# The first attention block of a four-layer kernel: queries and keys before the values' weights, values behind the first scores

## The reference, cut to what matters

```python
def _L0_attn_ref(x, Wq, Wk, Wv):
    ...
    Q = (x @ Wq.T).reshape(b, n, H, R)
    K = (x @ Wk.T).reshape(b, n, H, R)
    V = (x @ Wv.T).reshape(b, n, H, d)
    attn = jnp.einsum('bnhr,bmhr->bhnm', Q, K)
    attn = jax.nn.softmax(attn, axis=-1)
    out = jnp.einsum('bhnm,bmhd->bnd', attn, V)
    return out
...
x = x + _layernorm(_L0_attn_ref(_layernorm(x, axis=-1), ...), axis=-1)
x = x + _layernorm(_L0_ffn_ref(_layernorm(x, axis=-1), ...), axis=-1)
```

## Time and profile before

| | us |
|---|---|
| median of 3 runs | 1325.25 |
| lowest and highest | 1322.7, 1328.19 |
| the profiled execution | 1323.63 |
| its span in the trace | 1321.8 |
| first attention without a break on PE from | 52.9 |

### The profile page before, as it was taken

How to read it: one execution, slowest core, us unless ns; L and a number is a source line. 1 busy time by engine, 2 the same in 40 slices (tenths; PEclk the granted TensorE clock), 3 DMA queues, 4 the chain that set the end, 5 groups by cost and what they waited for, 6 DMA issues and landing times.

```text
span 1321.8 us, 21970 instructions
## 1 busy us (share of the span) xinstructions
PE 1196.8 (91%) x7921; PEld 686.2 (52%) x7921; DVE 994.1 (75%) x2058; ACT 799.6 (60%) x1585; POOL 386.1 (29%) x304
## 2 busy tenths in 40 slices
PE   6799999999999879895899999998889979799987
PEld 4366666666666634341333333343467754477653
DVE  5878978889879178777667677776689857888855
ACT  5876866767768123240466666676668862688751
POOL 0000000001000034474310000014588841698823
PEclk9899999999999989996699999998989989899999
DMA  5576857767768635562223321100111100011101
GB/s 153 127 168 151 184 136 171 168 150 159 171 139 186 155 107 129 140 193 72 76 59 96 83 43 42 39 3 22 28 29 30 36 20 0 21 34 34 30 13 32
DMA packets 62823, 119.92 MB, mean 91 GB/s; under 512 B 15522, under 2 KB 30060, under 8 KB 61324
## 3 DMA queue, kind: packets, MB, share of 16 engines
q1 hardware_dynamic: 62716, 118.53, 37.5%
HBM read 37.68 MB, written 5.57 MB: 33 GB/s over the span
## 4 chain that ended last, share of the span: by engine, by line
PE 71%; DVE 15%; ACT 5%; issue 4%; POOL 2%; DMA 2%; SPq 2%; DVEq 0%; POOLq 0%; ACTq 0%
PE ps L748 15%; PE ps L768 8%; PE ps L1068 6%; PE ps L1027 5%; PE ps L1048 4%; PE ps L1125 4%; PE ps L719 2%; PE ps L1176 2%; PE ps L1259 2%; PE ps L1198 2%; PE ps L1230 2%; ACT probsT L2257 2%; PE ps L900 2%; PE ps L1306 2%; PE ps L1241 2%
## 5 line engine op out<-in xcount | busy, mean ns | idle before, releaser
L2257 ACT ACTIVATE probsT<-ps 128x512 f32<-128x512 f32 (+1 forms) x304 | 163.9, 577 | 101.3 <-PE ps L1052 90.4
L1469 DVE TENSOR_REDUCE negmax<-ps 128x1 f32<-128x1024 f32 x128 | 153.6, 1205 | 40.0 <-PE ps L768 39.6
L2443 POOL TENSOR_SCALAR rstd<-mv 128x4 f32<-128x4 f32 (+1 forms) x31 | 7.9, 255 | 505.7 <-DVE mv L1403 505.4
L1027 PE MATMUL ps<-arena 84*128 84x512 bf16 (+3 forms) x384 | 114.9, 361 | 27.3 <-DVE cmax L1714 21.4
L768 PE MATMUL ps<-k_st,q_st 64*128 64x512 f32 x512 | 130.0, 627 | 9.7 <-ACT d_sq L2101 5.4
L2101 ACT ACTIVATE d_sq<-ps,negmax 128x1024 f32<-128x1024 f32 x86 | 96.0, 1116 | 61.4 <-DVE negmax L1469 58.7
L1714 DVE CUSTOM_DVE_ANT_0 q_st<-ps,rel 128x256 f32<-128x256 f32 (+7 forms) x128 | 96.7, 756 | 46.9 <-PE ps L1027 46.1
L1714 DVE CUSTOM_DVE_ANT_0 k_st<-ps,rel 128x256 f32<-128x256 f32 (+7 forms) x128 | 96.8, 756 | 38.7 <-PE ps L1027 37.7
L748 PE MATMUL ps<-probsT,v_nat 128*128 128x256 f32 x512 | 120.0, 388 | 5.2 <-DMA probsT<-probs 3.0
L748 PE MATMUL ps<-probsT,v_st 128*128 128x256 f32 x512 | 119.4, 385 | 0.8 <-DVE xn L1422 0.6
L1048 PE MATMUL ps<-arena 87*128 87x512 bf16 (+3 forms) x384 | 113.3, 338 | 5.5 <-ACT probsT L2257 3.3
(11 more groups left out here) (232 smaller groups left out, 2550.8 us busy)
## 6 DMA issues: line engine op xcount, KB each, us to landing
probsT<-arena SPq DMA_DIRECT2D x336, 128.0 KB, 2.4
probsT<-probs SPq DMA_DIRECT2D x176, 128.0 KB, 2.4
d_sq<-e_gates SPq DMA_DIRECT2D x16, 512.0 KB, 5.1
probsT<-probsT SPq DMA_DIRECT2D x62, 128.0 KB, 2.4
arena<-c_q_parts SPq DMA_DIRECT2D x8, 576.0 KB
arena<-c_k_parts SPq DMA_DIRECT2D x8, 576.0 KB
q_st<-e_gates SPq DMA_DIRECT2D x8, 512.0 KB, 5.1
k_st<-e_gates SPq DMA_DIRECT2D x8, 512.0 KB, 5.6
```

The lines of the kernel that those rows point to most:

```text
L1027: ins = pe.matmul(ps[:, 2 * (u % 2) + i, 0:e - i * CH], c_q2[buf][0:SHALLOW, j, qt * P:(qt + 1) * P], c_k2[buf][0:SHALLOW, j, i * CH:e], s ...
L1469: dve.tensor_reduce(negmax[:, u:u + 1], s2, AX_X, ALU.max, negate=True).then_inc(s_a_negmax, 1)
L2257: act.activation(c_p[:, kt % 2, j0:j0 + heads, q0 - kt * P:q0 - kt * P + n], ps[:, 4 + c % 2, 0:heads * n].rearrange("p (h n) -> p h n", n ...
```

## The change

The first block's order is new, all else of the kernel is untouched.

- PE no longer transposes Wv ahead of the projections. It projects the keys, then the queries, and goes to `scores(0, 0)`.
- `turn_w0(2)` and `(3)` move into the piece of slot 0, behind `scores(0, 0)`. The values' projection is split in halves, behind `scores(0, 1)` and `scores(0, 2)`; both halves go to banks 6 and 7, the second after the first is copied out.
- The scores of slots 0 and 1 of block 0 no longer wait for the values.
- `turn_f` moves: groups 0 to 3 all into slot 3, groups 4 to 7 all into slot 4, group 8 into slot 5. Group 0 also waits for the values' second half to be copied.
- DVE loses its two copies of the turned Wv and its copy of the values' second half. ACT makes them: the turned Wv in slot 0, the halves of the values in slots 1 and 2, the experts' copies in slots 3, 4 and 5.

```diff
                 if g == 0:
                     pe.wait_ge(s_ld_f, 16 * 11)
+                    pe.wait_ge(s_a_v1, 1)
...
-            def a_proj_v(m):
+            def a_proj_v(m, halves=(0, 1)):
                 b, p = m // PAIRS, m % PAIRS
-                if m > 0:
-                    pe.wait_ge(s_a_exp, NU * m)
-                for half, done in ((0, s_a_projv0), (1, s_a_projv1)):
-                    if half:
-                        pe.wait_ge(s_a_q, m + 1)
+                for half in halves:
+                    if m == 0:
+                        pe.wait_ge((s_w0t, s_a_v0)[half], (2, 1)[half])
+                    else:
+                        pe.wait_ge((s_a_exp, s_a_q)[half], (NU * m, m + 1)[half])
...
# PE: a_piece
-                if slot < 4:
-                    turn_f(2 * slot)
-                    turn_f(2 * slot + 1)
-                if slot == 4:
+                if slot == 0:
+                    pe.wait_ge(s_ld_wv, 16)
+                    turn_w0(2)
+                    turn_w0(3)
+                if slot in (1, 2):
+                    a_proj_v(0, (slot - 1,))
+                if slot in (3, 4):
+                    for g in range(4 * slot - 12, 4 * slot - 8):
+                        turn_f(g)
+                if slot == 5:
                     turn_f(8)
...
-            pe.wait_ge(s_ld_wv, 16)
-            turn_w0(2)
-            turn_w0(3)
             pe.wait_ge(s_w0a, 2)
             pe.wait_ge(s_xT, 2)
+            a_proj_k(0)
             a_proj_q(0)
-            a_proj_k(0)
-            pe.wait_ge(s_w0t, 2)
-            a_proj_v(0)
...
# DVE
-            turned_w0(0)
-            turned_w0(1)
             a_evac_k(0)
-            a_evac_v(0)
...
# ACT
+            def first_v(half):
+                act.wait_ge((s_a_projv0, s_a_projv1)[half], 1)
+                act.copy(a_v[0][:, 4 * half:4 * half + 4, :].rearrange("p (n k) c -> p n (k c)", n=2),
+                         ps[:, 6:8, :]).then_inc((s_a_v0, s_a_v1)[half], 1)
...
-                if slot < 4:
-                    turned_f(2 * slot)
-                    turned_f(2 * slot + 1)
-                if slot == 4:
+                if slot == 0:
+                    turned_w0(0)
+                    turned_w0(1)
+                if slot in (1, 2):
+                    first_v(slot - 1)
+                if slot in (3, 4):
+                    for g in range(4 * slot - 12, 4 * slot - 8):
+                        turned_f(g)
+                if slot == 5:
                     turned_f(8)
```

More of the change, by code:

```diff
@@ L708, in a_proj_k @@
                 ins.then_inc(s_a_projk, 1)
-            def a_proj_v(m):
+            def a_proj_v(m, halves=(0, 1)):
                 b, p = m // PAIRS, m % PAIRS
-                if m > 0:
-                    pe.wait_ge(s_a_exp, NU * m)
-                for half, done in ((0, s_a_projv0), (1, s_a_projv1)):
-                    if half:
-                        pe.wait_ge(s_a_q, m + 1)
+                for half in halves:
[3 more added lines that the diff above has]
+                        pe.wait_ge((s_a_exp, s_a_q)[half], (NU * m, m + 1)[half])
                     for i in range(4):
                         t = b * QT + 4 * half + i
-                        ins = pe.matmul(ps[:, pair(m, 2 + half) + i // 2, (i % 2) * 256:(i % 2) * 256 + 256],
+                        ins = pe.matmul(ps[:, (pair(m, 2 + half) if m else 6) + i // 2, (i % 2) * 256:(i % 2) * 256 + 256],
                                         xT[:, t * P:(t + 1) * P], w0v[:, p, :], start=True, stop=True)
-                    ins.then_inc(done, 1)
+                    ins.then_inc((s_a_projv0, s_a_projv1)[half], 1)
             def weigh(m, c, head, k0, k1):
@@ L757, in scores @@
                 if i == 0:
-                    for ready in (s_a_q, s_a_k, s_a_v0):
+                    for ready in (s_a_q, s_a_k):
                         pe.wait_ge(ready, m + 1)
+                    if m > 0:
+                        pe.wait_ge(s_a_v0, m + 1)
                 elif i == 1:
-                    pe.wait_ge(s_a_v1, m + 1)
+                    if m > 0:
+                        pe.wait_ge(s_a_v1, m + 1)
                     pe.wait_ge(s_a_exp, NU * m + 1)
@@ L1433, in half_xn @@
                 ins.then_inc(s_xn, 1)
[L1435 to L1439, removed]
             def a_evac_k(m):
@@ L2091, in a_evac_v, with turned_w0 @@
                 act.wait_ge(s_a_projv0, m + 1)
-                act.copy(a_v[m % 2][:, 0:4, :].rearrange("p (n k) c -> p n (k c)", n=2), ps[:, pair(m, 2):pair(m, 2) + 2, :]).then_inc(s_a_v0, 1)
+                act.copy(a_v[m % 2][:, 0:4, :].rearrange("p (n k) c -> p n (k c)", n=2),
+                         ps[:, pair(m, 2):pair(m, 2) + 2, :]).then_inc(s_a_v0, 1)
+            def first_v(half):
+                act.wait_ge((s_a_projv0, s_a_projv1)[half], 1)
+                act.copy(a_v[0][:, 4 * half:4 * half + 4, :].rearrange("p (n k) c -> p n (k c)", n=2),
+                         ps[:, 6:8, :]).then_inc((s_a_v0, s_a_v1)[half], 1)
+            def turned_w0(n):
+                act.wait_ge(s_w0p, 3 + n)
+                act.copy(w0v[:, 2 * n:2 * n + 2, :], ps[:, 6 + n, :].rearrange("p (n c) -> p n c", n=2)).then_inc(s_w0t, 1)
             def soft(m, u):
```

## The result

The changed kernel takes 1332.87 us (median of 9 runs), the kernel before 1323.26 (9 runs, the three shown above among them). The ratio is 1.0059, with a 95% interval of 1.0044 to 1.0074: slower by some 7.8 us (5.8 to 9.8).

A forecast was written before the change was run, and what follows sets the result against it. PE bounds the kernel (busy 91%), so only the first weighing's start counts: 5.6 for the holds net of the start's gain plus 2.8 for the clock make 8.4 us slower, 1325.25 + 8.4, rounded 1333.5, range 1329 to 1337.

The forecast's parts named there:

- The one number: The whole effect is how much the start of the first weighing, at 52.88 us before, moves.
- The premise: From the first weighing on, PE has work at every moment, and the change leaves that work as it is.
- The start: Projections up to the first scores: these start at 16.5 instead of 19.19 us, a gain of 2.7.
- Slots 0 to 2: The values' halves delay scores by 0.4 and 0.65, both covered; exponential of unit 6 at 35.0, gain still 2.7.
- Slots 3 and 4, the holds: PE waits for ACT's end-of-slot copies; scores of slots 4 and 5 start late; 5.3 lost by the exponential of unit 10.
- Slot 5: The weighing waits for the last small copies at the end of ACT's slot 5 and starts at 58.5 us.
- The sum without the clock: First weighing 5.6 us later if PE's clock stays at its upper level throughout.
- The clock: Two score bursts behind the idle times in slots 3 and 4 start at the lower clock: 2.8 us more.
- The upper bound: Clock cost if both bursts in slots 3 and 4 run low to their ends: 4.5 us.
- The clock did not stay up: Rival: holds in slots 3 and 4 but full clock, 5.6 us slower, 1330.9 us; chance 0.24.
- The gain at the start did not pass through: Rival claimed it would: slot 4's scores before about 37 us, first weighing 2.7 earlier, 1322.5 us; chance 0.07.
- The start did come forward: Rival claimed it would not: first scores stay where they were, 11.1 us slower, 1336.4 us; chance 0.05.

The follow-up runs named there:

- e2: The changed kernel with ACT's copies of the experts' groups moved forward in slot 4 alone: 1327.88 us, ratio 1.0022 to the kernel before.
- e5: e1 plus three matmuls that nobody reads in PE's idle time ahead of the scores of slot 6: 1320.16 us, ratio 0.9959 to the kernel before.
- e1: The changed kernel with ACT's copies of the experts' groups moved forward inside slots 3 to 5: 1322.28 us, ratio 0.9988 to the kernel before.
- e4: The changed kernel with matmuls that nobody reads in PE's idle time ahead of groups 2 and 6: 1328.67 us, ratio 1.0028 to the kernel before.

## Why the prediction was right, point by point

- **The one number.** All rests on the start of the first weighing. It moved by 8.5 (8.9 counted from PE's first transpose), the time by 7.8, forecast 8.4. That the forecast of 1333.5 lies 0.6 from the median is in part luck: it was built on 1325.25, 2.0 above the nine-run median of before, and the medians differ by 9.6.
- **The premise** that PE has work at every moment from the first weighing on is too strong. It is idle for 3.2 us of the next 340 and for 102.4 us of the rest of the span; in the changed kernel for 3.6 and 103.3. What the sum needs is only that this part doesn't change, and no run here shows that it did.
- **The start.** Forecast 2.7 at the first scores. The profile shows 3.0 net of the loads, the experiments 2.5 to 3.4 where the clock was up. The term that I had not counted is what the clock does to the start. In two of eight profiles of kernels with the new start the keys' projection took 3.75 instead of 1.95 (e2 and e5), and the gain there is only 0.9 and 0.4. The clock record begins with the rise to full speed, at 15.8 and 16.0 us in these two and at 9.6 to 11.4, ahead of the projection, in the other six. In the one profile of before it is at 12.3, just as the projections begin, so whether the old order escapes this isn't shown; nor is it shown that the 0.77 for which PE is now idle ahead of the projection plays a part, since all eight have it.
- **Slots 0 to 2.** As forecast: PE held by the values twice, no delay on ACT, exponential of unit 6 at 34.35 (forecast 35.0, 0.4 of the difference being the loads).
- **Slots 3 and 4, the holds.** Scores of slot 4 at 41.34 (41 to 42), of slot 5 at 52.44 (50 to 53), both ended by ACT's copies. e1 took the holds away and 9.4 us of time with them; e2 showed that each is half.
- **Slot 5.** The weighing at 61.40 stands 0.34 behind the start of ACT's last small copy (61.06), as in e2 (59.25 to 59.58), where that copy alone ended its wait. The scores of slot 6, low clock and all, ended at 61.35 and hid, barely.
- **The sum without the clock** was 5.6; e4 shows 5.4. With the 3.5 of the clock that makes the 8.9 of the profile, where 8.4 were forecast.
- **The clock** was the term that was too small: 2.8 taken, 3.5 measured. I had counted the low clock on the two score groups alone; the rows that I had left at full clock, the transposes released by the hold, cost 1.4 of it (0.83 + 0.61), while the second score group cost 0.83 and not 1.5. Two slips change nothing in the forecast. The upper bound takes 0.85 for six transposes where the row has 0.93. And the 1.6 and 1.7 by the Trainium skill (TensorE: Matmul & The Clock Gate, HAM oscillation) halve the whole rows of 3.26 and 3.49, where the page halves the throttled time. Of the first row only the 2.7 us from 39.56 to 42.25 are that, which gives 1.3, as measured.
- **The rivals.** The clock did not stay up. The gain at the start did not pass through: its point of decision was a start of slot 4's scores before about 37, it was 41.34. The start did come forward.

## What to carry to other kernels

When side work is packed closer on an in-order engine, look at its buffers: with two banks, the third and fourth group wait for copies of the same batch, and then everything queued behind them starts at the copier's pace. Place a copy in its engine's order by when the other engine needs the buffer back, not at the end of a stage; that alone took away the 7.8 us of loss here, and 1.6 to 2.4 of gain are left by the ratios, whose intervals end at 1.0000. And count the clock when a hold leaves TensorE idle: here the transposes and scores behind the two holds (3.96 and 5.35 us idle) ran low for the most part, which added 3.5 us to the 5.4 that the kernel would have lost at full clock.

## What the runs showed of the hardware

Matmuls that nobody reads, put into TensorE's idle time, paid: with them the granted clock stayed at 1.00 through both holds, and 3.5 us were won without moving one dependency. They have to end in time: in e5 a filler that began late held back the scores behind it. The projection at the start took 1.95 or 3.75 us for the same four records, though PE's order up to it is the same in all eight kernels with the new start. The difference goes with the first entry of the clock record, at 11.4 us at the latest or at 15.8 and 16.0.
